# The expert stage of a four-block kernel written out for its eight rounds, with a new order of work on every engine

## What is computed

```python
x = x + tanh(g_xattn[1]) * L1_xattn(ctx, ctx, layernorm(x))   # y = conv(k*v pairs, ssm_kernel), times q
x = x + tanh(g_ffn[1]) * L1_ffn(layernorm(x))
# L1_ffn, xf = layernorm(x) as 4096 x 512:
gate = xf @ Wg + bg;  w = softmax over the 6 best of 8
g = einsum('td,ndh->tnh', xf, Wgate) + bgate      # 6 routed experts, 256 hidden each
u = einsum('td,ndh->tnh', xf, Wup) + bup
h = silu(g) * u
routed = sum_n w_n * (h_n @ Wdown_n + bdown_n)
share = silu(xf @ Ws_up + bs_up) @ Ws_down + bs_down   # 512 hidden
out = routed + share
```

## Time and profile before

| | us |
|---|---|
| three timed runs | 2332.95, 2332.93, 2327.42 |
| median | 2332.93 |
| the profiled execution, own time | 2325.81 |
| its span in the trace | 2324.0 |
| from the span's start to the end of the attention and feed-forward blocks | about 804 |
| opening (x read, convolution of the first rows alone) | about 142 |
| rounds 0 to 6, measured from `up(g, 0)` to `up(g + 1, 0)` | 180.7, 175.9, 176.2, 177.3, 177.3, 177.5, 176.0 |
| round 7 (without a next convolution) | 129.8 |
| last additions and store | 7.5 |

### The profile page before, as it was taken

One profiled execution on the slowest core, in us unless ns is written; L12 is line 12 of the kernel. 1 busy time (PEld: TensorE's weight loads), 2 busy tenths in 40 slices (PEclk: granted clock), 3 DMA queues, 4 the chain that ended last, 5 costly groups with the idle time before them and its releaser, 6 DMA issues.

```text
span 2324.0 us, 30136 instructions
## 1 busy us (share of the span) xinstructions
PE 2017.0 (87%) x10162; PEld 1602.5 (69%) x10162; DVE 1546.4 (67%) x2487; ACT 1017.7 (44%) x1414; POOL 952.0 (41%) x775
## 2 busy tenths in 40 slices
PE   5999568887787545799899899899899899899998
PEld 4989444444454234688788788788788788688787
DVE  4776456666666358588578678678578579578511
ACT  3345345555555321633633633633633633443432
POOL 0110133333332021465465465465465465365464
PEclk9999779999999857899999999999999999899999
DMA  6666314443443321322332332332232242232231
GB/s 214 235 217 231 131 54 116 111 105 96 108 118 82 69 66 46 104 85 90 111 95 86 109 103 86 106 106 86 93 119 82 80 124 90 72 113 73 69 136 64
DMA packets 169968, 248.76 MB, mean 107 GB/s; under 512 B 91280, under 2 KB 92688, under 8 KB 163632
## 3 DMA queue, kind: packets, MB, share of 16 engines
q1 hardware_dynamic: 169616, 247.86, 34.3%
q10 hardware_dynamic: 288, 0.10, 0.0%
HBM read 193.26 MB, written 33.69 MB: 98 GB/s over the span
## 4 chain that ended last, share of the span: by engine, by line
PE 43%; DVE 7%; issue 6%; ACT 5%; POOL 3%; DMA 1%; ACTq 0%; SPq 0%; DVEq 0%; POOLq 0%
PE e_ps_u L54 4%; PE e_ps_u L56 4%; PE e_ps_u L55 4%; PE e_ps_m L54 4%; PE e_ps_m L56 3%; PE e_ps_m L55 3%; PE e_ps_out L54 3%; PE e_ps_out L55 3%; PE e_ps_out L56 3%; PE e_ps_g L56 3%; PE e_ps_g L55 3%; PE e_ps_g L54 3%; POOL e_dn_lo L1185 1%; DVE e_kv_lo L1504 1%; DVE e_x3T L1532 1%
## 5 line engine op out<-in xcount | busy, mean ns | idle before, releaser
L1180 POOL TENSOR_TENSOR e_gu_lo<-e_gu_raw,e_gu_hi 128x1024 fp32r<-128x1024 f32 (+1 forms) x128 | 272.8, 2131 | 449.6 <-ACT e_gu_hi L1269 447.3
L1532 DVE TENSOR_REDUCE e_x3T<-e_zp 128x128 f32<-128x1024 f32 x128 | 267.4, 2089 | 4.4
L54 PE MATMUL e_ps_u<-e_xn_hi,e_gu_hi 128*128 128x512 f32 x512 | 205.5, 401 | 4.0 <-DVE e_xn_lo L1554 2.5
L54 PE MATMUL e_ps_out<-e_hd_hi,e_dn_hi 128*128 128x512 f32 x512 | 208.8, 408 | 0.0
L54 PE MATMUL e_ps_m<-e_kv_hi,e_t_hi 128*128 128x288 f32 x592 | 180.7, 305 | 29.7 <-DVE e_kv_lo L1504 22.1
L55 PE MATMUL e_ps_out<-e_hd_lo,e_dn_hi 128*128 128x512 f32 x512 | 205.2, 401 | 0.0
L56 PE MATMUL e_ps_out<-e_hd_hi,e_dn_lo 128*128 128x512 f32 x512 | 205.2, 401 | 0.0
L55 PE MATMUL e_ps_u<-e_xn_lo,e_gu_hi 128*128 128x512 f32 x512 | 203.7, 398 | 0.0
L56 PE MATMUL e_ps_u<-e_xn_hi,e_gu_lo 128*128 128x512 f32 x512 | 203.6, 398 | 0.0
L958 PE MATMUL ps_h<-w1q,ayqT 128*128 128x512 bf16 x512 | 130.3, 403 | 79.4 <-ACT ah L681 71.9
L1203 POOL TENSOR_TENSOR e_kv_raw<-e_ke 128x512 f32<-128x512 f32 x128 | 139.4, 1089 | 125.7 <-DVE e_kv_lo L1504 95.5
(11 more groups left out here) (271 smaller groups left out, 5304.7 us busy)
## 6 DMA issues: line engine op xcount, KB each, us to landing
e_gu_raw<-in_mgu SPq DMA_DIRECT2D x96, 512.0 KB, 3.3
e_dn_raw<-in_md SPq DMA_DIRECT2D x128, 256.0 KB, 3.2
e_wb<-wts SPq DMA_DIRECT2D x8, 1536.0 KB, 6.6
stage<-in_x SPq DMA_DIRECT2D x8, 1024.0 KB, 6.8
c<-in_ctxT SPq DMA_DIRECT2D x8, 1024.0 KB, 5.8
raw_w<-in_w1T SPq DMA_DIRECT2D x8, 1024.0 KB, 4.8
raw_w<-in_w2T SPq DMA_DIRECT2D x8, 1024.0 KB, 7.3
gates<-gate SPq DMA_DIRECT2D x8, 1024.0 KB, 4.8
```

Source lines behind the costliest of these rows:

```text
L54: nc.tensor.matmul(out, w_hi, x_hi, start=first, stop=False, skip_group_check=skip)
L1180: nc.gpsimd.tensor_tensor(gu_lo[:, s % 2, a], gu_raw[:, s % 2, a], f32(gu_hi[:, s % 2, a]), ALU.subtract).then_inc(gulo_done, 1)
L1532: nc.vector.tensor_reduce(x3T[:, lb].rearrange("p (b n) -> p b n", b=B)[:, :, hh * CD:(hh + 1) * CD], zv(5, (1, 8), (21, 8)), AX.X, ALU.ad ...
```

## The change

The loops are gone. Every engine has one list of calls that Python writes out for the rounds, through a helper `at` that leaves a call out when its round does not exist:

```diff
-    UNITS = {2: [0], 3: [1], 4: [2, 3], 5: [4, 5], 6: [6], 7: [7, 8], 8: [9, 10], 9: [11], 10: [12, 13], 11: [14, 15]}
+    def at(op, c, *which, since=0):
+        if since <= c < NCH:
+            op(c, *which)
...
-        with nc.Fori(0, NCH - 1, engines=(mybir.EngineType.PE,), hint_back_edge=True) as g:
-            round_(g, g + 1)
-        round_(NCH - 1, None)
+        for i in range(-1, NCH + 1):
+            at(down, i - 1, 15)
+            at(turn_x2, i + 1, 0)
+            at(up, i, 0)
+            at(logits, i)
+            at(turn_x2, i + 1, 1)
+            at(up, i, 1)
+            at(turn_lg, i)
+            at(turn_q, i + 1, 0)
+            for k in range(3):
+                at(down_first, i, k)
+            at(turn_q, i + 1, 1)
+            at(up, i, 2)
+            at(down_first, i, 3)
+            at(down, i, 1)
+            at(unit, i + 1, 0)
+            at(turn_w, i)
...
+            at(unit, i + 1, 6)
+            at(gate, i, 7)
+            at(unit, i + 1, 7)
...
+            at(unit, i + 1, 10)
+            at(gate, i, 10)
+            at(unit, i + 1, 11)
...
+            at(gate, i, 15)
+            at(up, i, 15)
+            at(turn_xn, i + 1, 0)
+            at(down, i, 13)
+            at(bias, i)
+            at(turn_xn, i + 1, 1)
+            at(down, i, 14)
```

A unit on VectorE is split into `multiply` and `add_terms`, `finish` into its four columns, `route` into `route` and `weights`; the variance is taken by an aggregation instruction; `down(0)` becomes `down_first`, column by column:

```diff
-            variance(nc, dve, stats, mom, ve[:], LN_EPS, mom_done, 6 * q)
+            for j in range(TJ):
+                nc.vector.bn_aggr(mv[:, j], stats[:, j]).then_inc(mom_done, 1)
+            dve.wait_ge(mom_done, 5 * q + 4)
+            nc.vector.tensor_scalar(ve[:], mv[:, :, 1], LN_EPS, None, ALU.add).then_inc(mom_done, 1)
...
+        def down_first(g, k):
+            if k == 0:
+                pe.wait_ge(hdlo_done, START + STEPS * g + 1)
+                pe.wait_ge(dnlo_done, START + STEPS * g + 1)
+            if g > 0:
+                pe.wait_ge(y_done, START + 4 * (g - 1) + k + 1)
```

More of the change, by code:

```diff
@@ L1336, in cut_kv @@
             nc.scalar.activation(kv_hi[:, u % KT], kv_raw[:, u % 2], ACT.Copy).then_inc(kvhi_done, 1)
[L1338 to L1345 removed]
         def norm_nat(q, a):
             act.wait_ge(pshift_done, 2 * q + a + 1)
+            if q == 0:
+                act.wait_ge(setup_lo, 2)
             act.wait_ge(xnT_filled, START + 2 * q)
@@ L1463, in gated @@
         def gated(g, s):
-            if not routed(s):
-                return
             n = STEPS * g + s
@@ L1731, in turn_q, with unit @@
             last.then_inc(q_filled, 1)
-        def unit(q, u, after, out=ps_m[:]):
+        def unit(q, u):
             hh, lb = u // KT, u % KT
             v = CHD * KT * q + u
-            if u > 0 and after is None:
-                after = (prod_done, START + 4 * v)
+            out = first[u % 2] if q == 0 else ps_m[:]
             units = out.rearrange("p a (b n) -> p (a b) n", n=64)
@@ L1789, in _ @@
             pe.sem_inc(s, START)
-        turn_x2(0, 0, (x2T_done, START))
-        turn_x2(0, 1, (x2T_done, START + 1))
-        turn_q(0, 0, (x2T_done, START + 2))
-        turn_q(0, 1, (qe_done, START + 2))
-        for u in range(CHD * KT):
-            unit(0, u, (qe_done, START + 4) if u == 0 else (prod_done, START + 4 * (u - 1)), first[u % 2])
-        pe.wait_ge(setup_lo, 2)
-        pe.wait_ge(setup_hi, 2)
-        turn_x3(0, 0, (prod_done, START + 4 * CHD * KT))
-        turn_x3(0, 1, (xnat_done, START + 2))
```

727 lines of the change are left out of this document (447 added, 280 removed).

## The result

The changed kernel takes **2246.12 us** in the median of four runs (2245.67 to 2248.92), the kernel before 2332.66 in the median of four (2327.42 to 2332.95): a ratio of 0.9637, with a 95% interval of 0.9620 to 0.9653. The prediction said 2260 (2246 to 2296). The sign and the main mechanism held (TensorE is the bound, and the order of work takes its waits away). The time came out 14 us lower, 0.1 us above the lower end of the range, so that it lies inside by luck: four runs of one kernel differ by more. The profiled execution took 2245.67 us, with a span of 2243.6.

A forecast was written before the change was run, and what follows sets the result against it. TensorE was taken as the bound, with a floor of 166.3 us a round. Parts summed to 80 us, rounds to 79; less 7, 72 go, so 2253.8 profiled, plus 7.1 for the median: 2260 us, range 2246 to 2296.

The forecast's parts named there:

- The bound: From 946 us on TensorE bounds the kernel; a new order gives back only its waits and slow running.
- The turn, 42 us: Round end, turn_xn(1) waiting for VectorE's read: 29.5 us of waits and 12.6 of lower clock go, covered by products between turns.
- The queries, first unit and units, 28 us: TensorE's waits at turn_q(1), behind cut_kv and behind the multiplications go: 6 us for queries, 22 for the units.
- Leaving the loop, 6 us: Round 6, behind ScalarE's loop: TensorE's 4.1 us wait and 2 us of slow running go.
- First round and last, 2 and 2 us: Round 0, slowed by normalizing the second x, gives back 2 us; round 7 gives back 2.
- The opening, zero between -4 and +5: 846 to 946 us, VectorE sets the pace: 4 us gained by new places against later normalization; taken as 0.
- The aggregation at zero: Eight aggregations per round replace 18 small operations; taken as zero because they lie under TensorE's products.
- The transfers at zero: New places on SP for all transfers cost nothing: weights asked two steps ahead, next x and ctx needed 50 us later.
- How far I trust it, 7 us: Deduction of 1 us per round because some of six places with 0.4 to 1 us of room will fail.
- Rival A: Small margins at units fail when VectorE's subtractions are held beside GpSimd: 38 us saved, 2295 us, chance 0.2.
- Its second version, 2317 us: Rival A with VectorE waiting for a whole 2.4 us GpSimd instruction: the three places cost 50 us instead of 28.
- B and C: B: code comes too late on all engines, 2553 us, chance 0.04. C: queues out of step, 2333 us, chance 0.04.

The follow-up runs named there:

- Cover alone: Kernel after, but TensorE does down(13) and bias ahead of the first turn, so the two turns stand back to back: 2271.11 us, ratio 0.9753.
- the order on ScalarE and VectorE: Kernel after with TensorE's new order, but the next x's shift, normalization and GpSimd's root ahead of the turned xn's first cut: 2259.05 us, ratio 0.9697.
- both old together: Kernel after with ScalarE, VectorE and GpSimd's old turn order, and TensorE's down(13) and bias ahead of the turns, down(14) between: 2256.22 us, ratio 0.9685.
- the whole old round end: Kernel after with the old turn on all engines, plus the old statistics order, skip term, Toeplitz cut and small variance operations: 2274.41 us, ratio 0.9769.
- the run with one cover less: Kernel after, but TensorE does unit 11 right behind unit 10 and the gate of step 10 only then: 2263.68 us, ratio 0.9715.
- The additions: Kernel after with one or two unused two-input VectorE additions ahead of each unit's multiplications, except in the opening: 2316.83 us with one, 2406.57 with two.
- the added statistics: Kernel after with one unused VectorE statistics operation, reading one tile, ahead of each unit's multiplications except in the opening: 2253.78 us, ratio 0.9672.

## Why the prediction was right, and where it was off

**The bound: right.** "Gives back only what TensorE stands still or runs slowly": rounds 0 to 6 gave back 78.4 us, where the prediction had 77 to be had, and the last round 2.6 of 2. TensorE has one wait of 0.8 us left and, from 950 us on, the full clock.

**The turn, 42 us: gone, but mis-sized and wrong in why.** The losses of the earlier trace rows are gone. The 29.5 us of the earlier trace rows are not seven rounds: six of the waits (25.7 us) stand in rounds 0 to 5, the seventh (3.86 us) stands in the opening, where 2.46 us of it remain, and round 6 has none. With the slow products behind six of them, at 1.8 us each, the term is about 36 us and not 42. It did no harm, since the forecast went by the length of the rounds and not by the sum of the parts. The prediction gave the credit to the cover. Cover alone is worth 25 us in the new frame, the order on ScalarE and VectorE 13, both old together 10, and the whole old round end 28. A price of a part holds only in the frame in which it is taken. What failed in the reasoning is the reading of the earlier trace rows: the 1.24 us of the "small operation" was taken for its price, and the sentence that the rows show no hold was wrong. The operation takes 0.16 us, and the rest is the hold beside GpSimd. In the new order that cost the forecast nothing, since the shift is held there too (1.25 us in the timeline of after).

**The queries, first unit and units, 28 us: right as far as shown.** The list of waits has none of them left. (The rows' waits in the rounds are 51 us and not 52, which changes nothing.) For the units the run with one cover less shows the mechanism at its forecast price. Queries and first unit were not tested apart.

**Leaving the loop, 6 us: right**, 5.6 measured. Back edges at zero: right.

**First round and last, 2 and 2 us:** round 0 is 1.35 us above a steady one and was 4.5 above, so 3.1 went; the last gave 2.6.

**The opening, zero between -4 and +5:** it gained 4.1, at that end of the bound, and the execution took it back in the unchanged stage ahead of it.

**The aggregation at zero:** the reason, that it lies under TensorE's products, can hold only in the new order; in the old it is worth 11.6 us, mostly by a hold that it avoids. What it is worth in the new order wasn't tried. It takes 0.25 us for two and 0.38 for four in the trace of after.

**The transfers at zero:** TensorE never waits for one, but ScalarE does, 4.7 to 4.8 us in each of rounds 0 to 4 and 5.8 in round 5, so that this zero had no room to spare.

**How far I trust it, 7 us: too much.** This is half of the miss, and the term that was mis-sized. All places with less than 1 us of room held, in all seven rounds, and rounds 1 to 4 repeat to 0.01 us, with held operations of VectorE up to 2.5 us long in them. What failed instead was a place with 2.0 us of room, once in seven rounds, and it cost 1 us in all. The prediction had not listed it. A lateness of 0.95 us and a hold of 1.94 us together were more than its room. The floor of 166.3 us was 0.45 too high as well, but rounds 0 and 5 lie above it, so that this adds only 1.6 us. The other half is the step from the profiled execution to the median: 7.1 us added, as before, and 0.45 were due. The late attention stage of that execution, 4.7 us, is probably most of this; it is one execution of each kernel.

**Rival A: wrong in size for this kernel, its mechanism right.** Its sign, a wait of about 1 us at the same place in each round, is not there, but its mechanism struck once, in round 5. The additions show how near it was: margins of 0.9 us against holds of 0.4 to 1.5. Its second version, 2317 us, took holds of 2.4 us and left out the restarts of 0.25 us that the first has; with them it would be about 2322. Holds up to the end of a GpSimd instruction are what the rows show, 1.94 us in round 5; that they met only one place without enough room is the merit of this order. **B and C:** no TensorE wait for code or for a queue. The costliest groups on the page of after does show ScalarE with 43.6 us of "issue" in front of `e_gu_hi`, which the prediction had named as a sign of B. It isn't code: the longest, 3.95 us, ends at 1315.71, with the last product of `up(4)` (1315.23 + 0.39), for which that cut has to wait.

## What to carry to other kernels

Where one engine is the bound and an order repeats, take its floor as the forecast and no blanket deduction for thin margins; check each against the longest duration of the row ahead of it instead, and add how late that row can come. Before paying for a short operation on VectorE with two inputs in SBUF, look what GpSimd does at that moment: if GpSimd's instruction has begun, the price is the operation's own time plus the rest of that instruction; if VectorE begins first, GpSimd pays. So a place that is safe by 0.7 us of head start is safe only until something makes VectorE later, as round 5 and the added statistics show. And restore parts together as well as singly before giving credit to one of them.
